# Three PSUM banks in turn, in place of two, for the first pass of a quantised MLP on Trainium2

## What is computed

```
def quant_act_uint8(x):
    s = maximum(max(x), EPS) / 255.0
    return clip(round(x / s), 0.0, 255.0) * s

h = relu(quant_linear(layernorm(x), w1, b1))      # 256 -> 1024
x = x + quant_linear(h, w2, b2)                   # 1024 -> 256
```

## Time and profile before

| | |
|---|---|
| Time, three runs | 1225.44, 1228.97, 1229.59 us; median 1228.97 |
| Profiled execution | 1228.96 us, its span 1227.0 us |
| Granted TensorE clock, mean | 0.975 |
| Busy over the span | PE 92%, PEld 70%, DVE 68%, ACT 48%, POOL 50% |
| The first pass of the quantised MLP | from about 338 to 382.5 us of the span |
| The second pass | from about 387 to 449 us |

### The profile page before, as it was taken

The page is one execution under the profiler, slowest core; times in us unless marked ns, Lnnn a source line. Parts: engine busy times, 40 slices in busy tenths (PEclk is TensorE's granted clock), DMA queues, the critical chain, the costliest instruction groups (busy, mean ns, idle before and its releaser), DMA issues. The chain is left out here.

```text
span 1227.0 us, 27780 instructions
## 1 busy us (share of the span) xinstructions
PE 1123.4 (92%) x9978; PEld 857.4 (70%) x9978; DVE 839.3 (68%) x2661; ACT 585.3 (48%) x1056; POOL 612.8 (50%) x678
## 2 busy tenths in 40 slices
PE   1699999999687989999979999999999999999995
PEld 0245544544343658777869888889998989998995
DVE  6999999998778952347645795557656666565653
ACT  1488887877654742244157333324333333343431
POOL 4888777877246949994000027731333323232323
PEclk9999999999898999999969999999999999999998
DMA  9788879877212026630477043338889989898884
GB/s 268 137 179 169 179 165 163 155 161 241 84 58 69 1 87 214 198 120 0 139 210 187 1 153 129 128 125 270 268 272 268 278 265 270 270 266 266 270 256 94
DMA packets 180762, 215.71 MB, mean 176 GB/s; under 512 B 91936, under 2 KB 163488, under 8 KB 168112
## 3 DMA queue, kind: packets, MB, share of 16 engines
q1 hardware_dynamic: 163552, 193.75, 54.6%
q0 software_dynamic: 13296, 16.92, 7.0%
q10 hardware_dynamic: 3808, 3.67, 0.9%
HBM read 143.86 MB, written 50.38 MB: 158 GB/s over the span
## 5 line engine op out<-in xcount | busy, mean ns | idle before, releaser
L2223 PE MATMUL banks<-moe_w,moe_hT 128*128 128x256 f16 x2472 | 278.7, 273 | 0.0
L2223 PEld LDWEIGHTS banks<-moe_w,moe_hT 128*128 128x128 f16 x2472 | 241.6, 98 | 27.9
L2134 ACT ACTIVATE moe_hf<-banks,moe_b 128x256 f32<-128x256 f32 (+1 forms) x440 | 178.9, 458 | 167.9 <-PE banks L2210 166.9
L2078 POOL DMA_INDIRECT out_x<-moe_y,slot_owner x71 | 114.6, 1614 | 259.5 <-DMA out_x<-moe_y,slot_owner 182.2
L749 DVE CUSTOM_DVE_ANT_0 masked<-banks,mask_bias 128x256 f32<-128x256 f32 x512 | 185.9, 420 | 22.3 <-PE banks L571 18.4
L2210 PE MATMUL banks<-moe_rT,moe_w 128*128 128x256 f16 (+1 forms) x1872 | 192.8, 263 | 0.0
L2210 PEld LDWEIGHTS banks<-moe_rT,moe_w 128*128 128x128 f16 x1872 | 169.6, 98 | 17.1
L481 ACT ACTIVATE probsT<-banks 128x1024 f32<-128x1024 f32 x128 | 130.8, 1022 | 48.7 <-PE banks L602 48.7
L2330 DVE TENSOR_TENSOR moe_hT<-moe_hf,moe_hT 128x512 f16<-128x512 f32 (+1 forms) x220 | 145.5, 661 | 7.6
L571 PE MATMUL banks<-kT,qT 48*128 48x256 f16 x512 | 92.0, 285 | 42.0 <-DMA qT<-q_split 22.3
L2064 POOL DMA_INDIRECT slots_x<-moe_xn,pos x64 | 64.8, 1013 | 120.8 <-DVE pos L2408 101.6
(11 more groups left out here) (354 smaller groups left out, 1816.5 us busy)
## 6 DMA issues: line engine op xcount, KB each, us to landing
moe_w<-moe_halves SPq DMA_DIRECT2D x80, 1024.0 KB, 5.3
moe_halves<-half_parts SPq DMA_DIRECT2D x18, 1024.0 KB, 6.0
slots_x<-empty_row SPq DMA_DIRECT2D x1, 9230.0 KB, 43.2
moe_rows<-slots_x SPq DMA_DIRECT2D x32, 260.0 KB, 6.1
half_rows<-in_L_ffn_Wfc SPq DMA_DIRECT2D x8, 1024.0 KB, 8.6
half_rows<-in_L_ffn_Wproj SPq DMA_DIRECT2D x8, 1024.0 KB, 8.5
moe_b<-in_L_ffn_bproj SPq DMA_DIRECT2D x39, 128.0 KB, 6.2
ctx_rows<-in_ctx SPq DMA_DIRECT2D x16, 256.0 KB, 3.1
```

The source lines that it names most:

```text
L2078: pool.indirect_dma_start(out=out_rows, out_offset=bass.IndirectOffsetOnAxis(ap=owner[:, s, t:t + 1], axis=0), in_=y[s % 2][:, t, :], in_o ...
L2134: ins = act.activation(hf[p][:, j, 0:width], src, ACT.Gelu_apprx_tanh, bias=b1[buffer][:, j:j + 1], scale=1.0 / WSCALE)
L2223: ins = pe.matmul(OUT[p][:, t * D:(t + 1) * D], hT[p][:, x, j, t * P:(t + 1) * P], w2[buffer][:, w, j, :], start=(j == 0 and (w, x) == PAR ...
```

## The change

The pairs of the first pass take `banks[0]`, `banks[2]` and `banks[1]` in turn; the last one stays in `banks[3]`. Each pair from 3 on waits for the maximum of the pair three before it. Pair 1, the first in `banks[2]`, waits for the copy at L1272, for which VectorE now increments `m_uv` a second time; pair 2, the first in `banks[1]`, takes over the wait for all copied weights. The half pair that is computed again in `banks[2]` gets a wait for the maximum of pair 28, the last one that used this bank.

```diff
--- before.py
+++ after.py
@@ -947,7 +947,7 @@
         m_pm = sem("x_then_h_part_max_ready")
         m_am = sem("x_then_h_all_max_in_psum")
         m_ab = sem("x_scale_ready")
-        m_uv = sem("x_first_rounded")
+        m_uv = sem("x_first_rounded_then_sw2_copied")
         m_ua = sem("x_rounded_by_scalar")
         m_up = sem("x_rounded_by_pool")
         m_t = sem("xu_transposed")
@@ -972,7 +972,7 @@
         HID = (banks[1], banks[0], banks[3])
 
         def max_bank(n):
-            return banks[3] if n == NC * PAIRS - 1 else banks[n % 2]
+            return banks[3] if n == NC * PAIRS - 1 else banks[(0, 2, 1)[n % 3]]
 
         SPLIT = [n for n in range((NC - 1) * PAIRS) if n % 2 == 1 and n > 1]
 
@@ -1158,10 +1158,14 @@
 
             def for_max(c, jp):
                 n = c * PAIRS + jp
-                if n < 2:
-                    pe.wait_ge(m_wc, 2 * (n + 1))
+                if n == 0:
+                    pe.wait_ge(m_wc, 2)
+                elif n == 1:
+                    pe.wait_ge(m_uv, 2)
+                elif n == 2:
+                    pe.wait_ge(m_wc, 4)
                 elif n < NC * PAIRS - 1:
-                    pe.wait_ge(m_m, n - 1)
+                    pe.wait_ge(m_m, n - 2)
                 if n not in SPLIT:
                     return first_linear(max_bank(n), c, jp, m_f)
                 pe.wait_ge(m_d, c + 1)
@@ -1183,6 +1187,7 @@
                         columns(c + 1)
 
             last = banks[2]
+            pe.wait_ge(m_m, (NC - 1) * PAIRS + 1)
             first_half(last[:, 0:CW], NC - 1, 0)
             pe.wait_ge(m_pm, 2)
             pe.matmul(banks[2][:, 512:512 + P], ones[:], top_diag[:], start=True, stop=True).then_inc(m_am, 1)
@@ -1270,6 +1275,7 @@
 
             v.wait_ge(m_bc, 1)
             link(v.tensor_copy(sw2_bc[:], banks[2][:, 0:D]))
+            v.sem_inc(m_uv, 1)
             link(v.tensor_scalar(scale1[:], sw1[:], s_in[:, 0:1], None, ALU.mult))
             link(v.reciprocal(rscale1[:], scale1[:]))
             link(v.tensor_tensor(tmpj[:], b1[:], rscale1[:], ALU.mult))
```

## The result

The changed kernel takes 1221.98 us, median of 9 runs (1218.4 to 1225.72); the kernel before, 1230.09 us, median of 9 runs (1223.83 to 1237.02). The ratio is 0.9929, 95% interval 0.9904 to 0.9953: some 8.7 us less, with 5.8 to 11.8 inside the interval. The forecast was 1222.3, 6.7 us less. The profiled execution took 1221.38 us with a span of 1219.2, against 1227.0 before, at nearly the same mean clock (0.976).

What follows compares the result with a forecast made beforehand. The turn of one bank, banks[1], 2.66 us for two pairs, was taken to bound the first pass. Pass -7.0 and tail +0.3 gave -6.7 us, 1222.3 from 1228.97; range 1219.8 to 1226.0.

Steps and rivals of the forecast that it cites:

- The limit before: First pass, steady part: the turn of banks[1] sets the pace, 2.66 us for two pairs, 5.32 a chunk.
- The gain of the pass: First pass: its last reduce ends at 375.5 us in place of 382.53, a gain of 7.0 us.
- The two-chunk loop: First pass: from split fill through ScalarE's rounding and VectorE's reduces to a later fill, 8.33 us for two chunks, was 10.64.
- The start: First pass: pairs 0 to 3 run as now, first fills at half clock; pair 5 starts at about 345.15 us.
- x_step's 4.03: First pass: the loop of transposes, columns, GpSimd's subtraction and split fill takes 4.03 us a chunk.
- the wait behind the rounding: ScalarE, first pass: excess of pair 4c+3 waits for the rounding, about 0.3 us in every second chunk.
- The tail: After the last reduce: GpSimd's cutting ends 3.7 us later in place of 2.25, holding VectorE's chain; +0.3 us.
- The upper bound: Tail: VectorE's L1300 held until GpSimd's cutting is over, at 379.3 us, some 1.5 later than now.
- The small edits: Moved waits, added increment on VectorE and wait of the recomputed half pair: covered by idle time, cost nothing.
- rival 1: After the pass: full tail of 1.5 us and 0.9 at half speed given back, 1225.4 us; chance 0.10.
- Rival 2: First pass: third bank brings nothing, ScalarE's or VectorE's order keeps the pace at 2.66; 1228 to 1229 us; chance 0.06.
- Rival 3: First pass: TensorE stops often over three banks, clock falls to 1.2 GHz; slower, 1246 us; chance 0.04.

Runs made afterwards that it cites:

- run 1: The changed kernel's three banks, but each pair waits again for the maximum of the pair two before it; 1230.26 us, ratio to the kernel before 0.9991.
- run 4: The kernel before with ScalarE rounding one tile a chunk in place of two, GpSimd three; 1228.55 us.
- run 5: The kernel before with no split pairs, every pair whole; 1225.07 us, ratio to the kernel before 0.9962.
- run 3: The changed kernel with ScalarE rounding three tiles a chunk in place of two, GpSimd one; 1225.42 us.
- run 8: The changed kernel with ScalarE's excess of pair 4c+3 put ahead of the rounding; 1218.62 us.
- run 7: The changed kernel with two of GpSimd's four cutting pieces put off to the start of pass two; 1220.36 us.
- run 2: The changed kernel with ScalarE rounding one tile a chunk in place of two, GpSimd three; 1223.65 us.
- run 10: The changed kernel with a second, half-sized, unread subtraction ahead of each x_step on GpSimd; 1227.08 us.
- run 11: The changed kernel with two of GpSimd's four cutting pieces put off to the end of pass two; 1216.57 us.
- run 6: The changed kernel with no split pairs, every pair whole; 1223.28 us, ratio to the kernel before 0.9945.
- run 9: The changed kernel with TensorE's transposes one pair earlier and ScalarE's columns ahead of the excess of 4c+1; 1215.94 us.
- run 12: The changed kernel with transposes one pair earlier and two cutting pieces at the end of pass two; 1219.83 us, ratio to the kernel before 0.9916.

## Why the prediction was right

**The limit before** was as read. Run 1 gives the run-ahead back and the gain is gone; run 4 eases ScalarE's work and changes nothing; run 5 shortens the bank's turn and gains, at more work for VectorE.

**The gain of the pass** was forecast at 7.0 us and is 8.55. Two terms make the difference.
- The two-chunk loop was put at 8.33 and measures 8.10. The rounding holds ScalarE's next instruction back 0.98 us, not its full 1.08; a reduce with L1296 behind it takes 1.14, not 1.18; the handover to TensorE is 0.10, not 0.15. The 1.18 was already misread: it is 4.71 / 4, while the row gives (4.71 - 1.22) / 3 = 1.16 for the distance of two reduces. Over first to last excess this is 0.7 us (24.17 against the 24.9 of the worked schedule).
- The start came 0.72 us sooner by the first excess. No part of the change did that: the clock rose sooner. Before, it stood at half for 4.9 us from the first matmul; after, for 2.9. In the earlier trace rows the eight first matmuls take 3.59 us, after the change 3.32, and pair 3 is filled 4.46 us after the first matmul in place of 5.44. This is chance of the execution, as the other runs show: runs 3 to 8 have 3.59 again, and run 7, whose pass is that of the changed kernel, comes to its first excess in 6.45 us; run 1, which gives the run-ahead back, has 3.24 and 5.72. Without it the pass gains some 7.8.

**Where the step was wrong.** The text took the long loop for the only limit, so that x_step's 4.03 had slack, and expected the wait behind the rounding in every second chunk only. The wait is there in every chunk, since two such loops run interlaced; x_step's loop came out at 4.05 and its slack at nothing. The step that failed is setting 8.33 / 2 = 4.17 against 4.03 as if the 0.14 between them were more than the rows could carry. That the time was right all the same is in part because the two came out equal, so that it didn't matter which one was followed. Runs 2 and 8 show that easing ScalarE's loop alone gives nothing, run 3 that lengthening it costs, and run 10 that lengthening x_step's costs in full (0.63 us a chunk for 0.62).

**The tail** was forecast 0.3 longer and is 0.12 shorter, though GpSimd's cutting ends 4.05 us after the last reduce (forecast 3.7). The upper bound, L1306 held until the cutting is over, didn't happen: it was held no longer than the one GpSimd instruction beside it ran, L142, until 376.65 (L1306 ends at 376.73). Run 7 removes GpSimd's work and prices the contention at 1.0 us. The Trainium skill (SBUF — State Buffer, section Who interferes with whom) speaks of a hold for one instruction, so the 1.5 us that the prediction drew from it went beyond the page. What it says agrees for L1306 and for the reduces. Of an instruction with two SBUF inputs it says that it contends with a GpSimd one that reads SBUF; L1304, such an add, ends at 375.79 with L142 running on to 376.65, so it was slowed, 0.54 against 0.17, and not shut out until L142 was over.

**The small edits** cost nothing that shows, as forecast: the first reduce still waits 0.81 us for TensorE. The reduces and L1296 stay at 1.22 and 0.42 us with TensorE denser.

**Rivals.** Of rival 1, the full tail did not come, but TensorE does stand longer before L1193 (4.4 us in place of 3.5); the half-clock stretch that follows is 10.2 us long in both. Rival 2 is out by the 4.05. Rival 3 is out: the granted clock is 1.00 from 341.4 us to behind the last reduce; the Trainium skill's swinging clock (TensorE: Matmul & The Clock Gate, section A second HAM failure mode: psum-queue depth-cycling) is not seen in the changed kernel or in any of the twelve runs, whose granted clock from 345 to 370 us is 1.00 throughout.

Of the total, 8.7 us measured against 6.7 forecast, 1.6 are the pass (0.7 of it the start, which is chance) and 0.4 the tail, as the two traces have it; what the later blocks add or take lies within the noise, and so does the difference of 2 us itself.

## What to carry to other kernels

When a wait closes a loop through a buffer, write the loop as a sum of rows; if it adds up to the period to the hundredth, that buffer's turn is the limit, and the gain of another buffer goes down to the next loop. List all loops before you choose the next limit, and take two that differ by a few per cent as equal: easing one of them alone brought nothing here. A trick that spares one engine work (here the split pairs) can cost time while a buffer's turn is the limit and pay only once that limit is gone.

## What the runs showed of the hardware that was not expected

The time of TensorE at half clock differs between executions of the same work. Around the scale of the hidden layer the granted clock was 0.50 from 383.8 to 394.1 before and from 375.5 to 385.8 after, 10.2 us, but only for 6.8 us in run 8 (376.6 to 383.4), in run 11 (375.1 to 382.0) and as long in runs 1, 5, 6, 7, 9 and 12. What pass two takes goes with how much of that stretch lies behind L1098, and not evenly. Where it is 4.2 to 4.4 us (runs 5, 8, 9 and 11), L1098 to the next block's first matmul is 60.7 to 60.9 us. Where it is 5.7 to 7.3 us (before, after and runs 1 to 4, 6, 10 and 12), it is 61.9 to 62.3, and no longer with 7.3 than with 5.7. Why the one us more at half clock costs 1.0 to 1.6 us in all and the next ones nothing is open. And the first matmul of the pass comes anywhere from 336.1 us (run 5) to 341.0 (run 10), although neither edit touches the work ahead of it. Together that is more than most edits here are worth, and it is why a gain of 1 us is to be looked for between two marks of a trace and not in a total; even there the clock has to be laid beside it.
